# Preparing the second cross-attention's weights and first queries inside the latent stage of a decoder kernel

## Chip, cores and metric

The kernel runs on one core of one Trainium2 chip. The metric is the device time of one execution in microseconds, of which the median over the runs is taken.

## What is computed

Two decoder layers with a layer norm behind every sublayer, over 8 items of 112 tokens and 256 features, all in fp32. The stages in order: a state-space layer, a cross-attention of 16 heads, a mixture of experts, a latent attention, a wide cross-attention, and a last feed-forward with gated low-rank parts. The change touches the fourth and fifth:

```python
x = _layernorm(x + _L1_attn_ref(x, ...))      # latent attention, 16 heads of 16, causal
x = _layernorm(x + _L1_xattn_ref(x, ctx_768, Wq, Wk, Wv, Wo, bo))
x = _layernorm(x + _L1_ffn_ref(x, ...))

def _L1_xattn_ref(x, context, Wq, Wk, Wv, Wo, bo):   # context: 8 x 375 x 192
    q = (x @ Wq).reshape(B, Tq, 8, 128) * SCALE
    k = (context @ Wk).reshape(B, Tk, 8, 128) * SCALE
    v = (context @ Wv).reshape(B, Tk, 8, 128)
    attn = softmax(einsum('bqhc,bkhc->bhqk', q, k))
    return einsum('bqhk,bkhc->bqhc', attn, v).reshape(B, Tq, 1024) @ Wo + bo
```

## The kernel before, in words

Each stage is a function with one or two instruction blocks; at the end of a block all engines meet. Inside a block every engine has a program of its own and the engines wait for each other by counting semaphores. The order of work is written out by hand. The state lies in SBUF twice: `core.x` (tokens on partitions) and `core.xt` (features on partitions). There are eight PSUM banks of 512 fp32 columns.

**Latent attention** (`latent_attention`, L1881) has two blocks. The first (L1939 to L2015) makes latents, queries and keys with their rotations. SP sends queries and keys to DRAM and back into strips (`q_strips`, `k_strips`), one half of the items at a time (`rearrange`, L1905); GpSimd clears the strips first (L1942). The second block (L2040 to L2275) holds the attention in rounds: in round r TensorE makes the scores of item r+1 (banks 0 to 3, L2067 and L2073), turns the probabilities of item r (banks 5 and 6, L2086) and weighs its values (bank 7, L2095), and finishes item r−1: `turn_back` (L2102), `turn_output` (L2110), `out_projection` (L2115), all but the first in bank 4. `turn_state` (L2121) turns the normalized state of item r−2 back for `core.xt`. VectorE takes the maxima and subtracts them (`below_top`, L2161 and L2163), divides, adds the residual and normalizes (L2169 to L2190). ScalarE makes the exponentials (L2215), copies out of PSUM (L2220, L2225, L2230, L2241, L2247) and the deviation (L2235, L2236). Round −1 fills this pipeline, rounds 8 and 9 drain it. SP only sends the second half of the strips in this block, GpSimd sets the values' ones column and adds the output bias to the state (L2054).

**The wide cross-attention** (`wide_cross_attention`, L1057) multiplies no query or key projection per item. It folds the weights: per head, Wq times Wk turned into `w_a`, and Wv times Wo into `w_b`. For that the weights are turned first. TensorE prepares in two lists (L1073, L1074, run at L1313 and L1316):
- `first`: seven groups of turns (four of Wq, three of Wk), six groups of folds into `w_a` (L1192), and the six groups of the first queries (`w_a` times the state of items 0 and 1, L1222, by the helper at L86);
- then the first scores (`scores(0, 0)`, L1277 and L1280);
- `second`: three groups of turns of Wv (L1182), six groups of folds into `w_b` (L1201, L1205), and two groups of turns of the first context (L1225, L1228).

Each group fills one bank, alternately 0 and 7; ScalarE empties bank 0 (L1513, L1514) and VectorE bank 7 (L1375, L1376). A group is written only once the last one in its bank is copied. Then come 8 items of four units each (L1318). In a unit TensorE makes the scores of the following unit, turns probabilities (L1289) and does one or two small jobs in bank 0 (`jobs`, L1076): queries two items ahead, context turns, output projection (L1232), and the feed-forward's parts. VectorE makes the maxima (L1382) and normalizes; ScalarE makes the exponentials (L1521). GpSimd adds the output bias `bo` to the state at the stage's start (L1165), and VectorE waits for that (`bias_added`) before its first `normalize_heads`. SP loads two contexts, then the feed-forward's weights, then each further context two items ahead (L1151). The cross-attention weights themselves were loaded during the mixture stage (L1663).

The two-instruction count of fp32 matmuls in the rows (48 for 24 of them) is how the profile records them.

Of the kernel before, what the change touches and what calls it, by code (L numbers as in the profile page):

```python
# [7 lines left out]
F32 = mybir.dt.float32  # L8
# [8 lines left out]
N = B * T  # L17
# [13 lines left out]
INNER = 1024  # L31

# [97 lines left out]
class Core:  # L130
# [25 lines left out]
    def allocate_parts(self, ctx):  # L156
# [8 lines left out]
            {n: sbr(f"w{n}_{part}", [128, INNER]) for n in "kv"} for part in ("high", "low", "rest", "rest_low"))  # L165

# [890 lines left out]
def wide_cross_attention(core, d, output):  # L1057
# [44 lines left out]
    PRE = len(first) + len(second)  # L1102
    HALF = PRE // 2
    assert PRE % 2 == 0

    def pre_at(job_):
        return (first + second).index(job_)

    with ExitStack() as ctx:
        sb = lambda name, shape: ctx.enter_context(nc.sbuf_tensor(f"x{layer}_{name}", shape, F32))  # L1110
        pair = lambda name, shape: [sb(f"{name}{p}", shape) for p in range(2)]
        wq_t, wk_t, wv_t = sb("wq_t", [128, G, D]), sb("wk_t", [128, G, DC]), sb("wv_t", [128, G, DC])
        w_a, w_b = sb("w_a", [128, KD, M, 128]), sb("w_b", [128, M, D])
        ctx_t, cn = pair("ctx_t", [128, 2, SE]), pair("cn", [SP_, ST, DC])
        qt = pair("qt", [128, M, 2 * T])
# [7 lines left out]
        ctx_loaded = [sem("ctx_loaded0"), sem("ctx_loaded1")]  # L1123
        pre_ready, pre_used = [sem("pre_ready0"), sem("pre_ready1")], [sem("pre_used0"), sem("pre_used1")]
# [21 lines left out]
        PRE_BANK = [bank[0], bank[7]]  # L1146

        with nc.Block() as block:
            @block.sync
            def _(sp):  # L1150
                for i in range(B):  # L1151
                    if i == 2:
                        core.load_lora_weights(sp, d)
                    if i >= 2:
                        sp.wait_ge(s_ready, (i - 1) * J)
                    sp.dma_start(ctx_t[i % 2][:, :, :], d["ctx_t"][i].rearrange("(c p) n -> p c n", p=128)).then_inc(ctx_loaded[i % 2], 16)
# [12 lines left out]
            def _(pe):  # L1169
                ident = core.c(128, C_ID, 128)  # L1170

                def prepare(n, job_):

                    out, kind = PRE_BANK[n % 2], job_[0]
                    wait_past(pe, pre_used[n % 2], n // 2)
                    if kind == "turn":
                        _, name, c, g = job_
                        w = dict(q=core.wq, k=core.wk, v=core.wv)[name]
                        rows = 128 if name == "q" or c == 0 else CB
                        for k in range(512 // rows):  # L1180
                            h = 4 * g + k
                            last = pe.transpose(out[:, k * rows:(k + 1) * rows], w[0:rows, c, h * 128:(h + 1) * 128], ident[0:rows, 0:rows])  # L1182
                    elif kind == "fold_a":
                        _, c, g = job_
                        if c == 0 and g == 0:
                            for b in range(2):
                                pe.wait_ge(pre_used[b], (len(TURNS) + 1 - b) // 2)
                        cols = slice(0, 128) if g < 2 else slice(128, DC)
                        wide = cols.stop - cols.start
                        for k in range(512 // wide):  # L1190
# [3 lines left out]
                    elif kind == "fold_b":  # L1194
                        if job_[1] == 0:
                            for b in range(2):
                                pe.wait_ge(pre_used[b], (pre_at(job_) + 1 - b) // 2)
# [1154 lines left out]
```

## Time and profile before

| | |
|---|---|
| median of 3 runs | 1099.26 us (1098.34 to 1099.91) |
| profiled execution: its own time | 1098.13 us |
| its span in the profile | 1096.3 us |
| TensorE busy in the span | 998.7 us, 91% |
| VectorE, ScalarE, GpSimd busy | 586.3, 410.3, 150.6 us |
| mean granted clock of TensorE | 0.964 |

Times in the rows count from the span's start. In this execution the latent stage's first block begins near 671.1 us, its second near 694.4 us, and the wide cross-attention near 784.5 us. Busy time of TensorE is that of its matmuls, which overlap and whose ends are modelled; its granted clock is given as a share of 2.4 GHz, so 0.50 is 1.2 GHz. "Idle before" names what ended an engine's idle time.

### The profile page before, as it was taken

What the parts mean: (1) busy time and instruction counts of PE and PEld (TensorE: products, weight loads), DVE (VectorE), ACT (ScalarE), POOL (GpSimd) and SP (SyncE); (2) the same over time, 40 slices, a digit from 0 to 9 for tenths busy, and PEclk for the clock granted to TensorE, in tenths of its full rate; (3) what the DMA queues carried; (4) which work ended last, traced back from release to release, by engine and by line L of the source; (5) the groups of instructions that cost most, each with busy time, mean ns of one, the idle gap of its engine ahead of it and who ended that gap; (6) DMA issues with size and microseconds to landing.
All of it is one profiled execution on the core that took longest, in us unless ns stands there. A gap on an engine that the chain in (4) does not pass through costs nothing. (4 is left out here: it accounts for less than half of the span.)

```text
span 1096.3 us, 17961 instructions
## 1 busy us (share of the span) xinstructions
PE 998.7 (91%) x6656; PEld 773.7 (71%) x6656; DVE 586.3 (53%) x1319; ACT 410.3 (37%) x1065; POOL 150.6 (14%) x151
## 2 busy tenths in 40 slices
PE   6899699999999999869999996688789999999985
PEld 4578577777777777569999994355576776676563
DVE  2786545555555556656655554477325444544543
ACT  2556433333333334335444522366423222322221
POOL 0334311011011000014343422100100000000000
PEclk9999899999999999979999997899799999999997
DMA  4500000000000000074121000600100000001000
GB/s 146 186 2 1 29 15 1 16 15 1 14 0 0 0 0 0 1 242 117 46 70 38 0 1 1 135 1 2 46 1 15 15 15 15 14 2 27 4 6 13
DMA packets 24286, 34.34 MB, mean 31 GB/s; under 512 B 3168, under 2 KB 19888, under 8 KB 24224
## 3 DMA queue, kind: packets, MB, share of 16 engines
q1 hardware_dynamic: 24224, 33.51, 10.3%
q8 instruction: 39, 0.64, 0.2%
q14 instruction: 23, 0.19, 0.1%
HBM read 30.75 MB, written 2.75 MB: 31 GB/s over the span
## 5 line engine op out<-in xcount | busy, mean ns | idle before, releaser
L1028 ACT ACTIVATE x_prob<-bank,x_negmax 112x375 f32<-112x375 f32 x128 | 72.3, 570 | 153.2 <-DVE x_negmax L944 153.2
L1778 DVE TENSOR_TENSOR moe_h_low<-moe_sq,moe_h_high 128x448 fp32r<-128x448 f32 x64 | 54.8, 873 | 52.8 <-ACT moe_h_high L1843 39.6
L1819 POOL TENSOR_TENSOR moe_sq<-moe_r 128x448 f32<-128x448 f32 x64 | 64.2, 1005 | 122.3 <-ACT moe_r L1851 103.8
L86 PE MATMUL bank<-moe_w_low,moe_h_high 128*112 128x256 f32 x256 | 71.8, 281 | 0.0
L86 PE MATMUL bank<-moe_w_high,moe_h_high 128*112 128x256 f32 x256 | 71.7, 280 | 0.0
L86 PE MATMUL bank<-moe_w_high,moe_h_low 128*112 128x256 f32 x256 | 71.7, 280 | 0.0
L944 DVE TENSOR_REDUCE x_negmax<-bank 112x1 f32<-112x375 f32 x128 | 64.1, 543 | 7.7 <-PE bank L836 5.7
L1851 ACT ACTIVATE moe_r<-bank 128x448 f32<-128x448 f32 x64 | 35.0, 546 | 86.6 <-PE bank L86 84.9
L1521 ACT ACTIVATE x_prob<-bank,x_negmax 112x375 f32<-112x375 f32 x64 | 36.1, 569 | 76.4 <-DVE x_negmax L1382 76.4
L949 DVE COPY x_prob_t<-bank 125x336 f32<-125x336 f32 x128 | 59.0, 499 | 5.7 <-PE bank L845 3.8
L857 PEld LDWEIGHTS bank<-x_prob_t,x_v 125*64 125x64 f32 x768 | 37.2, 136 | 33.9 <-issue 29.9
L836 PE MATMUL bank<-x_kt,x_qt 64*112 64x375 f32 x256 | 56.8, 521 | 0.7 <-DVE x_kt L936 0.7
L845 PE MATMUL bank<-const,x_prob 112*125 112x112 f32 x384 | 53.7, 274 | 3.2 <-ACT x_prob L1028 3.0
L845 PEld LDWEIGHTS bank<-const,x_prob 112*125 112x125 f32 x384 | 50.3, 188 | 6.8 <-ACT x_prob L1028 5.4
L86 PE MATMUL bank<-moe_xt_high,moe_w_high 128*128 128x448 f32 x128 | 48.4, 378 | 4.2 <-DVE moe_w_low L1784 2.9
L86 PE MATMUL bank<-w_in,xt 128*112 128x512 f32 (+2 forms) x128 | 42.0, 467 | 11.1 <-DMA w_in<-in_L_attn_W_in 8.3
L857 PE MATMUL bank<-x_prob_t,x_v 125*64 125x112 f32 x768 | 50.8, 268 | 0.0
L810 POOL COPY x_inv<-x_inv_head 112x512 f32<-112x512 f32 x16 | 9.8, 615 | 281.5 <-DVE x_inv_head L955 281.5
L1277 PE MATMUL bank<-x_ctx_t,x_qt 128*112 128x375 f32 x128 | 46.7, 487 | 1.8 <-ACT x_prob L1521 1.0
L1382 DVE TENSOR_REDUCE x_negmax<-bank 112x1 f32<-112x375 f32 x64 | 32.1, 543 | 29.7 <-PE bank L1280 29.7
L86 PE MATMUL bank<-moe_xt_low,moe_w_high 128*128 128x448 f32 x128 | 47.4, 370 | 0.0
L86 PE MATMUL bank<-moe_xt_high,moe_w_low 128*128 128x448 f32 x128 | 47.3, 370 | 0.0
(360 smaller groups left out, 2281.0 us busy)
## 6 DMA issues: line engine op xcount, KB each, us to landing
moe_w<-in_L_ffn_W SPq DMA_DIRECT2D x16, 512.0 KB, 4.7
ctx_t<-in_ctx_t SPq DMA_DIRECT2D x8, 376.0 KB, 4.7
x_ctx_t<-in_ctx_t SPq DMA_DIRECT2D x8, 376.0 KB, 3.4
wk<-in_L_xattn_Wk SPq DMA_DIRECT2D x2, 1024.0 KB, 6.7
wv<-in_L_xattn_Wv SPq DMA_DIRECT2D x2, 1024.0 KB, 9.4
wq<-in_L_xattn_Wq SPq DMA_DIRECT2D x2, 1024.0 KB, 11.5
wo<-in_L_xattn_Wo SPq DMA_DIRECT2D x2, 1024.0 KB, 13.3
w_in<-in_L_attn_W_in SPq DMA_DIRECT2D x1, 1160.0 KB, 6.9
```

Source lines behind the costliest of these rows:

```text
L86: last = pe.matmul(out, lhs, rhs, start=(k == 0), stop=(k == len(pairs) - 1))
L836: last = pe.matmul(S_BANK(u, e)[0:T, 0:S], qt[p][rows, u, :], kt[p][rows, u, :], start=True, stop=True)
L845: last = pe.transpose(T_BANK(u, e)[0:SP_, k * T:(k + 1) * T], PROB(u, e)[:, k * SP_:(k + 1) * SP_], ident[0:T, 0:T])
L857: last = pe.matmul(bank[6 + u // HU][e * DH:(e + 1) * DH, at:at + T], v[p][:, k, g * DH:(g + 1) * DH], prob_t[u % 2][e][:, k, :], start=(k ...
L944: dve.tensor_reduce(negmax[:, g:g + 1], S_BANK(u, e)[0:T, 0:S], AX_X, ALU.max, negate=True).then_inc(max_ready, 1)
L949: dve.tensor_copy(prob_t[u % 2][e][:, :, :], T_BANK(u, e)[0:SP_, 0:ST * T] .rearrange("s (k t) -> s k t", k=ST)).then_inc(pt_copied, 1)
L1028: act.activation(PROB(u, e)[:, :], S_BANK(u, e)[0:T, 0:S], ACT.Exp, bias=negmax[:, g:g + 1], accum_out=total[:, g:g + 1]).then_inc(p_ready, 1)
L1277: pe.matmul(S_BANK[e][0:T, 0:S], q[:, 2 * j + e, query], c[:, 0, 0:S], start=True, stop=False)
L1521: act.activation(prob[w % 2][e][:, :], S_BANK[e][0:T, 0:S], ACT.Exp, bias=negmax[:, g:g + 1], accum_out=total[:, g:g + 1]).then_inc(e_read ...
L1778: dve.tensor_tensor(h_low[half][:, m, :], sq[m % 2][:, :], h_high[half][:, m, :].bitcast(F32), ALU.subtract).then_inc(low_done, 1)
L1819: pool.tensor_tensor(sq[m % 2][:, :], r[m % 2][:, :], r[m % 2][:, :], ALU.mult).then_inc(sq_done, 1)
L1851: act.activation(r[m % 2][:, :], bank[m][:, 0:HALF], ACT.Relu).then_inc(h_used, 1)
```

## The change

The turned and folded weights, both context tiles, the turned context and the first queries get a place that lasts over both stages (`allocate_folded`); the first queries lie in the memory of `q_strips`, which is dead behind the last latent scores. The two preparation lists and the two-bank scheme leave `wide_cross_attention`, which now starts with `scores(0, 0)`; its SP loads the feed-forward weights first and contexts from item 2 on. The latent stage gets 30 groups of extra work, numbered 0 to 29:
- 0 to 6, the turns of Wq and Wk: ahead of the second block's first scores, banks 5 and 6 in turn, copied by ScalarE (even numbers) and VectorE (odd);
- 7 to 12, the folds into `w_a`: in round 0, ahead of the scores of item 1, banks 5, 6 and 7 in turn, all copied by ScalarE, between its exponentials of item 0;
- 13 to 15, the turns of Wv: behind round 7's last weighing; 16 to 18 and 19 to 21, the folds into `w_b`: in round 8, before and behind `turn_output`; 22, 23 (first context) and 24, 25 (first queries) behind the last `out_projection`; 26 to 29, the other first queries, in round 9. All of these use banks 0 and 1, copied by ScalarE (even) and VectorE (odd).

The turn of the last item's state comes behind all of them. The two context loads are now the first thing that SP does in the latent stage's first block. The counts and shapes of the moved matmuls, turns and copies stay. The bodies of `prepare` and `empty_extra` are those of the removed functions and are left out where they say nothing of order.

```diff
+    def allocate_folded(self, ctx):
+
+        sb = lambda name, shape: ctx.enter_context(self.nc.sbuf_tensor("x1_" + name, shape, F32))
+        self.wq_t, self.wk_t, self.wv_t = sb("wq_t", [128, XG, D]), sb("wk_t", [128, XG, DC]), sb("wv_t", [128, XG, DC])
+        self.w_a, self.w_b = sb("w_a", [128, KD, XM, 128]), sb("w_b", [128, XM, D])
+        self.x1_ctx = [sb(f"ctx_t{p}", [128, 2, SE]) for p in range(2)]
+        self.x1_cn = [sb(f"cn{p}", [SP_, ST, DC]) for p in range(2)]
+        self.q_strips = ctx.enter_context(self.nc.sbuf_tensor("la_q_strips", [128, 4, N], F32))
+        self.first_queries = self.q_strips[:, :, :].rearrange("p g n -> p (g n)")[:, 0:XM * 2 * T].rearrange("p (m t) -> p m t", m=XM)
+        self.x1_ctx_loaded = [self.sem("x1_ctx_loaded0"), self.sem("x1_ctx_loaded1")]
...
-    TURNS = [("q", c, g) for c in range(KD) for g in range(2)] + [("k", 0, 0), ("k", 0, 1), ("k", 1, 0)]
-    FOLDS = [(c, g) for c in range(KD) for g in range(2)] + [(c, 2) for c in range(KD)]
-    first = [("turn", *t) for t in TURNS] + [("fold_a", *f) for f in FOLDS] + [(QUERY, 0, a) for a in range(6)]
-    second = [("turn", "v", 0, 0), ("turn", "v", 0, 1), ("turn", "v", 1, 0)] + [("fold_b", n) for n in range(6)] + [(CTX_MAIN, 0), (CTX_REST, 0)]
...
+        w_a, w_b, ctx_t, cn = core.w_a, core.w_b, core.x1_ctx, core.x1_cn
+        qt = [core.first_queries, sb("qt1", [128, M, 2 * T])]
...
-                for i in range(B):
-                    if i == 2:
-                        core.load_lora_weights(sp, d)
-                    if i >= 2:
-                        sp.wait_ge(s_ready, (i - 1) * J)
+                core.load_lora_weights(sp, d)
+                for i in range(2, B):
+                    sp.wait_ge(s_ready, (i - 1) * J)
...
-                    if number[job_] == 0:
-                        pe.wait_ge(pre_used[0], HALF)
-                    else:
-                        pe.wait_ge(job_used, number[job_])
+                    wait_past(pe, job_used, number[job_])
...
-                pe.wait_ge(core.xw_loaded, 80 * (layer + 1))
-                for n, job_ in enumerate(first):
-                    prepare(n, job_)
                 scores(0, 0)
-                for n, job_ in enumerate(second):
-                    prepare(len(first) + n, job_)
                 for i in range(B + 2):
                     for u in range(J):
...
-                def prepared(n, job_):
-                    if n % 2 == 1:
-                        dve.wait_ge(pre_ready[1], n // 2 + 1)
-                        empty(job_, PRE_BANK[1], copy).then_inc(pre_used[1], 1)
-
-                for n, job_ in enumerate(first):
-                    prepared(n, job_)
                 row_max(0, 0)
                 dve.wait_ge(bias_added, 1)
-                for n, job_ in enumerate(second):
-                    prepared(len(first) + n, job_)
                 normalize_heads(0, 0)
                 for i in range(B + 1):
                     for u in range(J):
...
                     act.wait_ge(end_log_ready, i + 1)
                     act.activation(end_rstd[:, i, :], end_rstd[:, i, :], ACT.Exp, scale=-0.5).then_inc(end_rstd_ready, 1)
...
                 act.preload_act_table_set(EXP_LN)
-                for n, job_ in enumerate(first):
-                    prepared(n, job_)
                 exps(0, 0)
-                for n, job_ in enumerate(second):
-                    prepared(len(first) + n, job_)
...
+                    for i in range(2):
+                        sp.dma_start(core.x1_ctx[i][:, :, :], d["ctx_t"][i].rearrange("(c p) n -> p c n", p=128)).then_inc(core.x1_ctx_loaded[i], 16)
                     sp.wait_ge(strips_cleared, 1)
...
+            turns = [("turn", "q", c, g) for c in range(KD) for g in range(2)] + [
+                ("turn", "k", 0, 0), ("turn", "k", 0, 1), ("turn", "k", 1, 0)]
+            folds = [("fold_a", c, g) for c in range(KD) for g in range(2)] + [("fold_a", c, 2) for c in range(KD)]
+            value_turns = [("turn", "v", 0, 0), ("turn", "v", 0, 1), ("turn", "v", 1, 0)]
+            value_folds = [("fold_b", n) for n in range(6)]
+            first = [("context", 0), ("context", 1)] + [("query", a) for a in range(6)]
+            extra = turns + folds + value_turns + value_folds + first
+            AHEAD, FILL = len(turns), len(turns) + len(folds)
+            TAIL_V, TAIL_F = FILL + len(value_turns), FILL + len(value_turns) + len(value_folds)
+
+            def place(n):
+
+                if n < AHEAD:
+                    return 5 + n % 2, ("act", "dve")[n % 2]
+                if n < FILL:
+                    return 5 + n % 3, "act"
+                return n % 2, ("act", "dve")[n % 2]
+
+            def evicted(engine, n):
+
+                return sum(1 for k in range(n) if place(k)[1] == engine)
...
+                    def wait_evicted(n):
+
+                        for engine in ("act", "dve"):
+                            wait_past(pe, pre_used[engine], evicted(engine, n))
+
+                    def prepare(n):
+
+                        job, (b, _) = extra[n], place(n)
+                        out = bank[b]
+                        if n == FILL:
+                            pe.wait_ge(m_ready, NG * B)
+                        before = [k for k in range(n) if place(k)[0] == b]
+                        if before:
+                            engine = place(before[-1])[1]
+                            pe.wait_ge(pre_used[engine], evicted(engine, before[-1] + 1))
+                        if n in (AHEAD, TAIL_V, TAIL_F):
+                            wait_evicted(n)
...
+                        elif job[0] == "query":
+                            if job[1] == 0:
+                                pe.wait_ge(nt_copied, 2)
...
+                        last.then_inc(pre_ready, 1)
+
+                    def prepare_all(a, b):
+                        for n in range(a, b):
+                            prepare(n)
+
+                    pe.wait_ge(core.xw_loaded, 160)
+                    prepare_all(0, AHEAD)
                     pe.wait_ge(wo_loaded, 48)
                     for r in range(-1, B + 2):
+                        if r == 0:
+                            prepare_all(AHEAD, FILL)
                         if there(r + 1):
                             scores(r + 1)
                         if there(r - 1):
                             turn_back(r - 1)
-                        if there(r - 2):
+                        if there(r - 2) and r <= B:
                             turn_state(r - 2)
+                        if r == B:
+                            prepare_all(TAIL_V, TAIL_V + 3)
+                        if r == 0:
+                            wait_evicted(FILL)
                         if there(r):
                             turn(r, 0)
                             turn(r, 1)
...
                             turn(r, 2)
                             weigh(r, 1)
                         if there(r - 1):
+                            if r == B:
+                                prepare_all(TAIL_V + 3, TAIL_F)
                             out_projection(r - 1)
+                            if r == B:
+                                prepare_all(TAIL_F, TAIL_F + 4)
                         if there(r):
                             turn(r, 3)
                             weigh(r, 2)
...
                             values(r + 1)
                         if there(r):
                             weigh(r, 3)
+                        if r == B - 1:
+                            prepare_all(FILL, TAIL_V)
+                        if r == B + 1:
+                            prepare_all(TAIL_F + 4, len(extra))
+                            turn_state(B - 1)
 
...
+                    empty_extras(0, AHEAD)
                     for r in range(-1, B + 1):
                         if there(r + 1):
                             below_top(r + 1, 0)
+                        if r == B:
+                            empty_extras(FILL, TAIL_V)
                         if there(r - 1):
                             divide(r - 1)
                         if there(r + 1):
                             below_top(r + 1, 1)
                             below_top(r + 1, 2)
                             below_top(r + 1, 3)
+                        if r == B:
+                            empty_extras(TAIL_V, TAIL_F)
                         if there(r - 1):
                             residual(r - 1)
                             normalize(r - 1)
+                    empty_extras(TAIL_F, len(extra))
...
+                    def empty_extras(a, b):
+                        for n in range(a, b):
+                            if place(n)[1] == "act":
+                                act.wait_ge(pre_ready, n + 1)
+                                empty_extra(n, copy).then_inc(pre_used["act"], 1)
+
+                    empty_extras(0, AHEAD)
                     for r in range(-1, B + 2):
                         if there(r - 1):
                             copy_weighed(r - 1)
-                        if there(r - 2):
+                        if r == B:
+                            empty_extras(FILL, TAIL_V)
+                        if there(r - 2) and r <= B:
                             copy_state(r - 2)
                         if there(r):
                             copy_turned(r, 0)
                         if there(r + 1):
                             exps(r + 1, 0)
+                        if r < 0:
+                            empty_extras(AHEAD, AHEAD + 1)
                         if there(r):
                             copy_turned(r, 1)
+                        if r == B:
+                            empty_extras(TAIL_V, TAIL_V + 3)
                         if there(r - 1):
                             copy_output(r - 1)
                         if there(r + 1):
                             exps(r + 1, 1)
+                        if r < 0:
+                            empty_extras(AHEAD + 1, AHEAD + 3)
                         if there(r):
                             copy_turned(r, 2)
                         if there(r + 1):
                             exps(r + 1, 2)
+                        if r < 0:
+                            empty_extras(AHEAD + 3, AHEAD + 4)
                         if there(r):
                             copy_turned(r, 3)
                         if there(r + 1):
                             exps(r + 1, 3)
+                        if r < 0:
+                            empty_extras(AHEAD + 4, FILL)
+                        if r == B:
+                            empty_extras(TAIL_V + 3, TAIL_F)
                         if there(r - 1):
                             deviation(r - 1)
                         if there(r + 1):
                             copy_values(r + 1)
+                        if r == B:
+                            empty_extras(TAIL_F, len(extra))
+                            copy_state(B - 1)
...
-        latent_attention(core, d)
-        wide_cross_attention(core, d, out)
+        with ExitStack() as second:
+            core.allocate_folded(second)
+            latent_attention(core, d)
+            wide_cross_attention(core, d, out)
```

## Rows read from the trace of the kernel before

**Rows 1.** The page, part 1: busy time, share of the span, instructions.

```profile
PE 998.7 (91%) x6656; PEld 773.7 (71%) x6656; DVE 586.3 (53%) x1319; ACT 410.3 (37%) x1065; POOL 150.6 (14%) x151
```

**Rows 2.** Windows by stage: length, busy us per engine, TensorE clock, DMA share, GB/s.

```profile
694.45:713.76 19.31, 12.34 (x125) 7.87 (x125) 9.44 (x16) 7.46 (x14) 5.18 (x5) 0.73 0.51 97
713.76:775.44 61.68, 53.09 (x650) 36.49 (x646) 42.67 (x103) 40.01 (x98) 0.00 (x0) 0.97 0.01 2
775.44:784.55 9.11, 3.94 (x14) 2.19 (x14) 2.74 (x10) 3.08 (x10) 0.00 (x0) 0.67 0.00 1
...
811.85:823.72 11.87, 10.04 (x56) 7.35 (x54) 4.37 (x7) 3.93 (x9) 0.00 (x0) 0.86 0.00 1
823.72:1096.30 272.58, 249.94 (x1275) 174.48 (x1274) 129.35 (x399) 72.84 (x252) 0.00 (x0) 0.97 0.05 13
```

**Rows 3.** Timeline of the wide stage's start: start, length, engine, line, operation.

```profile
784.58 4.52 POOL L1165 TENSOR_TENSOR x<-x,bo 112x2048 f32<-112x2048 f32 x1 [84.89 <-POOLq L2040]
784.59 3.87 PE L1182 MATMUL bank<-const,wq 128*128 128x128 f32 x16 [0.69 <-PEq L2040]
...
791.26 7.64 PE L1192 MATMUL bank<-x_wk_t,x_wq_t 128*128 128x128 f32 x64 [0.72 <-ACT x_wk_t L1513]
...
809.62 1.48 PE L1277 MATMUL bank<-x_ctx_t,x_qt 128*112 128x375 f32 x4 [0.67 <-issue]
...
811.97 1.00 DVE L1382 TENSOR_REDUCE x_negmax<-bank 112x1 f32<-112x375 f32 x2 [3.87 <-PE bank L1280]
...
813.11 0.57 ACT L1521 ACTIVATE x_prob<-bank,x_negmax 112x375 f32<-112x375 f32 x1
...
823.72 1.51 PE L1277 MATMUL bank<-x_ctx_t,x_qt 128*112 128x375 f32 x4
```

**Rows 4.** Timeline of the start of the latent rounds.

```profile
694.45 1.28 ACT L2209 ACT_TABLE_LOAD   x1 [0.27 <-PEq L1939]
...
696.62 1.71 PE L2067 MATMUL bank<-la_hide,la_ident 112*112 112x448 bf16 x4 [4.57 <-DMA la_k_strips<-la_keys]
...
700.18 0.62 DVE L2161 TENSOR_REDUCE la_top<-bank 112x4 f32<-112x448 f32 x1 [6.66 <-PE bank L2073]
...
705.09 1.74 PE L2067 MATMUL bank<-la_hide,la_ident 112*112 112x448 bf16 x4 [4.38 <-DVE la_masked L2163]
...
713.76 0.96 PE L2067 MATMUL bank<-la_hide,la_ident 112*112 112x448 bf16 x4
...
715.77 0.63 DVE L2161 TENSOR_REDUCE la_top<-bank 112x4 f32<-112x448 f32 x1 [2.24 <-PE bank L2073]
```

**Rows 5.** Timeline of the last weighing and the drain behind it.

```profile
775.04 0.40 PE L2095 MATMUL bank<-la_prob_t,la_v 112*32 112x112 f32 x8 [0.29 <-ACT la_prob_t L2220]
...
775.99 0.41 DVE L2190 TENSOR_SCALAR la_normed<-la_res,la_mv,la_rstd 112x256 f32<-112x256 f32 x1 [0.51 <-ACT la_rstd L2236]
...
776.43 0.65 PE L2102 MATMUL bank<-const,la_weighed 128*112 128x128 f32 x4 [0.99 <-ACT la_weighed L2225]
...
778.73 2.05 PE L86 MATMUL bank<-la_wo,la_ot 128*112 128x256 f32 x4 [0.43 <-ACT la_ot L2230]
...
782.50 0.20 ACT L2236 ACTIVATE la_rstd<-la_rstd 112x1 f32<-112x1 f32 x1
...
783.94 0.35 ACT L2247 COPY xt<-bank 128x224 f32<-128x224 f32 x1 [0.29 <-PE bank L2121]
```

**Rows 6.** Groups by form on TensorE, 784 to 824 us.

```profile
L86 PE MATMUL bank<-xt,x_w_a 128*128 128x224 f32 x48 | 9.3, 354 | 0.7 <-issue 0.7
...
L1192 PE MATMUL bank<-x_wk_t,x_wq_t 128*128 128x128 f32 x32 | 4.0, 280 | 0.7 <-ACT x_wk_t L1513 0.7
...
L1192 PE MATMUL bank<-x_wk_t,x_wq_t 128*128 128x64 f32 x32 | 3.8, 276 | 0.0
```

**Rows 7.** Windows of TensorE alone: length, busy us, clock, DMA share, GB/s.

```profile
812.00:816.00 4.00, 2.44 (x20) 1.00 0.00 0
816.00:819.00 3.00, 3.00 (x9) 0.50 0.02 5
```

More of the change, by code:

```diff
@@ L31 @@
 INNER = 1024
+XG = 8
+XM = XG + XG // 2
 E0, F0, FM = 8, 512, 4
@@ L1101, in wide_cross_attention @@
         number[job_] = len(number)
[L1102 to L1107, printed above, removed]
     with ExitStack() as ctx:
@@ L1145, in wide_cross_attention @@
         JOB, S_BANK, T_BANK, U_BANK = bank[0], bank[1:3], bank[3:5], bank[5:8]
-        PRE_BANK = [bank[0], bank[7]]
         with nc.Block() as block:
@@ L1170, in _ @@
                 ident = core.c(128, C_ID, 128)
[L1172 to L1190, printed above, removed]
-                            h = (4 * g + k) % G
-                            last = pe.matmul(out[:, k * wide:(k + 1) * wide], wq_t[:, h, c * 128:(c + 1) * 128], wk_t[:, h, cols],
-                                             start=True, stop=True)
[L1194 to L1197, printed above, removed]
-                        for k in range(2):
-                            at = 2 * job_[1] + k
-                            if at < G:
-                                last = pe.matmul(out[:, k * D:(k + 1) * D], wv_t[:, at, 0:128], core.wo[:, at, :], start=True, stop=True)
-                            else:
-                                for e in range(2):
-                                    h = 2 * (at - G) + e
-                                    last = pe.matmul(out[e * CB:(e + 1) * CB, k * D:(k + 1) * D], wv_t[:, h, 128:DC], core.wo[:, h, :],
-                                                     start=True, stop=True)
-                    else:
-                        if kind == QUERY and job_[2] == 0:
-                            for b in range(2):
-                                pe.wait_ge(pre_used[b], (n + 1 - b) // 2)
-                        if kind == CTX_MAIN:
-                            pe.wait_ge(ctx_loaded[0], 16)
-                        last = work(out, job_)
-                    last.then_inc(pre_ready[n % 2], 1)
@@ L1268, in scores @@
                         pe.wait_ge(ctx_loaded[i % 2], 16 * (i // 2 + 1))
-                        if i == 0:
-                            for b in range(2):
-                                pe.wait_ge(pre_used[b], (len(first) + 1 - b) // 2)
-                        elif i % 2 == 0:
+                        if i > 0 and i % 2 == 0:
                             pe.wait_ge(job_used, number[(QUERY, i // 2, 4)] + 1)
@@ L1296, in weigh @@
                     wait_past(pe, ot_dve, 2 * i + half)
-                    if i == 0:
-                        for b in range(2):
-                            pe.wait_ge(pre_used[b], HALF)
-                    elif half == 0:
+                    if i > 0 and half == 0:
                         pe.wait_ge(job_used, number[(CTX_MAIN, i)] + 1)
```

96 lines of the change are left out of this document (71 added, 25 removed).

## The prediction

> **What bounds the kernel now.** I read the page first: TensorE is busy 91% of the span [rows 1], so a gain can only come from its idle time or from time at its lower clock. The windows by stage say where that is [rows 2]. Behind 823.72 us the second cross-attention keeps TensorE busy 249.94 of 272.58 us, and nothing there is touched. In the latent stage's repeating rounds (713.76 to 775.44 us) it is busy 53.09 of 61.68 us. Ahead of the rounds it is busy only 12.34 of 19.31 us at a mean clock of 0.73, and in the drain behind the last round 3.94 of 9.11 us at 0.67. Then come 39.17 us (784.55 to 823.72 us) of preparation in the next stage, ahead of its first round. The reader is to see two holes beside a block of work that needs TensorE and depends on little.
>
> The timeline of that block [rows 3]: seven groups of turns until 790.54 us, six folds of the query weights (7.64 us), six first queries, the first scores at 809.62 us, then the value turns, value folds and context turns until the second scores at 823.72 us. The first softmax (maxima from 811.97 us, exponentials until 813.68 us) lies under the value turns. I take the second scores as the anchor: from there the code of the stage is the same in both kernels.
>
> **What goes.** Between the last weighing of the latent stage (it ends at 775.44 us [rows 5]) and the anchor lie 48.28 us. The sum compares this distance with the new one and charges the delay ahead of the rounds apart.
>
> **Ahead of the rounds: seven turns.** The set-up before the latent rounds ends as the one at 784.5 us does, with a ScalarE table load at 694.45 us [rows 4]; the turns follow at once, with the same two banks and the same pair of copying engines. I price them as they ran: from 784.59 to 790.54 us, 5.95 us [rows 3]. So the first scores leave at about 700.5 us instead of 696.62 us, where they had waited 4.57 us for the key strips [rows 4]: +3.85 us. The two context loads go ahead of everything on SP's queue, at the stage's very start, where SP would only wait for the strips to be cleared and then for the projections; nothing is late behind them, so I take 0.
>
> These first scores ran at the low clock, since TensorE had idled before them: 3.56 us from their start to VectorE's first reduction, against 2.01 us for the same work from 713.76 to 715.77 us at full clock [rows 4]. Six microseconds of turns stand before them now; in the old place such turns were enough, for the folds right behind them ran at their best pace from the first to the last [rows 3, 6]. I take the high clock, −1.55 us, and keep 0 as the other end.
>
> **Ahead of the second scores: six folds.** They take 7.64 us at full clock [rows 3, 6]. VectorE meanwhile works through the first item; in the old kernel TensorE waited 4.38 us for it [rows 4]. New order: scores until 702.6, values until 703.3, folds until 710.9 us, second scores straight behind, 2.0 us at full clock, first reduction at 712.9 us. VectorE's four steps and then the third scores follow as before: the old second scores left at 705.09 us and, slow too, gave the reduction its start 3.56 us later; from there to the third scores at 713.76 us it is 5.1 us. So the third scores leave at 718.0 us. **The front costs 4.2 us**; 5.8 us if the first scores stay slow. Bounds: 1 us if turns and folds hide better, 14 us if folds and both scores run at the low clock (7.6 and 3.1 us more). I take 4.2, since the row nearest in kind, the folds behind their own turns, was at the high clock. ScalarE alone empties these banks now, three of them in turn. In the old block two banks and two engines let the folds run without a break, so one engine with three banks should keep up; its exponentials slip by one copy, which nobody waits for, as the next item's maxima come only after 712 us.
>
> A rule is weighed here. The rows show 16 folds of 128 columns in 4.0 us and 16 of 64 columns in 3.8 us (each two instructions [rows 6]): half the columns bought almost nothing. The Trainium skill (TensorE: Matmul & The Clock Gate, section Back-to-back issue gap) gives a gap that falls with the columns; by it the narrow folds would cost half, and the front some 1.9 us less. The rows decide.
>
> **Rounds.** Nothing is added in rounds 0 to 6; I take 0. The old rounds had TensorE waiting for VectorE and ScalarE in short pieces, and these stay.
>
> **Behind the rounds.** Everything counts from T, the end of the last weighing. Work now in the drain:
> - value turns, value folds and context turns: as between the first and second scores, 10.04 us busy out of 11.87 us [rows 2]. This contains a fall of the clock to 0.50 from 816 to 819 us at least [rows 7]: the 3 us of work done in it would have taken 1.5 us at full clock, so it cost 1.5 us, which I leave in as the price of one such fall.
> - six first queries: 9.32 us [rows 6].
> - the drain's own steps at full clock: 0.65 us for turning the weighed values back (four transposes [rows 5]), estimated from it 0.4 us each for the two-transpose steps (state, output, last state), 1.0 for the output projection (2.05 us at the low clock): 2.9 us.
> - waits that this order makes. The third value turn waits for VectorE, which first normalizes item 6 (until T+0.96) and then copies: 0.6 us. The first query needs the bank that holds the context turns, whose copy ScalarE makes only behind the last deviation. That comes 1.92 us after the projection's end (780.78 to 782.70 us [rows 5]) and the copy 0.5 us more; 1.1 us of context turns cover part: 1.4 us idle.
> - last copy 0.35 and the stage's boundary 0.30 us (783.94 to 784.59 us [rows 3, 5]): 0.7 us with the semaphore.
> Sum: 10.04 + 9.32 + 2.9 + 2.0 + 0.7 = 25.0 us, so the second cross-attention starts at T+25.0 instead of T+9.1.
> Then its first scores (809.62 to 811.91 us, 2.29 us), and now bare the first softmax (to 813.68 us, 1.77 us behind the scores' end, and a semaphore), since nothing lies beside it: 4.1 us. Anchor at **T+29.1, against T+48.28: 19.2 us gained**. Bounds: 14 us with two more falls of the clock and slow queries at the start, 22 us with none. GpSimd's bias addition (4.52 us [rows 3]) was under 39 us of preparation; it ends 0.5 us behind the exponentials now, and VectorE's first normalization waits for it behind its queue; the turn that needs it comes 3.9 us after the anchor, so 0, and at most 0.5.
>
> **Sum.** −19.2 + 4.2 = −15.0 us. The profiled execution took 1098.13 us (span 1096.3), so 1083.1 us; the median of the runs is 1.13 us above it, which gives 1084.3 us.
>
> **Rivals.**
> 1. *The front runs at the low clock.* TensorE's turns there stop for copies, and the first two stand about 1 us until the table load is over. For it: the clock fell behind the value turns, in which TensorE had kept stopping for copies (busy 2.44 of the 4 us before the fall [rows 7]); against it: in the old block it rose behind the same turns. Price: folds +7.6, two scores +3.1: 1095 us. Beside it: the Trainium skill (same page, section A second HAM failure mode: psum-queue depth-cycling) says that pauses between groups that cycle through PSUM banks make the clock swing; the fall at 816 us agrees, and by this rule the time would lie between 1084 and 1095 us. Chance 0.12.
> 2. *The holes hide more.* The drain runs without a fall of the clock and the value turns fit round their copies (−3), and the folds start early (−1.5): 1080 us or a little less. For it: the fall at 816 us followed stalls for copies that the fuller order of the drain may cover. Chance 0.10.
> 3. *Slower.* The low clock holds through all the moved work, front and drain. The work is the same wherever it stands, so each microsecond of it that is run at 1.2 instead of 2.4 GHz takes one more; it decides from 15 us of such work. All of it (folds 7.6, scores 3.1, drain about 22) gives 1084 + 33 = 1117 us. Against it: the value work, stalls and all, had a mean clock of 0.86 in the old place [rows 2]. Chance 0.03.
> 4. *No change.* The rounds take the gain back, because ScalarE's late copies shift every exponential, 1.9 us in each of eight rounds. Against it: only round 0 holds added copies, and the later rounds' order is untouched. 1099 us, chance 0.02.
>
> **Numbers.** My case, a gain between 9 and 19 us, has 0.73. The range takes the price bounds of front and drain together, 1080 to 1090 us: it leaves out most of rivals 1, 3 and 4, some of rival 2. Against about 0.2% that a measurement of this kernel can tell, faster 0.95, same 0.02, slower 0.03.
>
> **What would show it.** The latent stage's first scores near 700.5 us and its third near 718; rounds of unchanged pace; from the last weighing 25 us to the next stage's table load; there the first scores at once, then 1.8 us idle on TensorE, and nothing changed behind the anchor. A mean clock under 0.9 from 702 to 713 us would be rival 1. Wrong altogether would be rounds that lengthen, or a gap on TensorE of over 2 us in the drain.

## The result and the profile after

The changed kernel takes 1088.70 us in the median of four runs (1081.28 to 1089.54), the kernel before 1099.41 us beside it: ratio 0.988, 95% interval 0.984 to 0.992. The forecast was 1084.3 us (1080 to 1090). The profiled execution of the changed kernel took 1089.54 us, with a span of 1087.7 us: 8.6 us less span than before, where 15.0 us was forecast.

The page, part 1, of the changed kernel, beside [rows 1]:

```profile
PE 1000.9 (92%) x6656; PEld 775.4 (71%) x6656; DVE 584.4 (54%) x1316; ACT 411.1 (38%) x1068; POOL 150.5 (14%) x151
```

The same number of TensorE instructions, 2 us more busy time in a shorter span: no work went away, and some of it ran slower. The windows by stage say where (columns as in [rows 2]):

```profile
0.00:673.05 673.05, 626.99 (x4338) 516.12 (x4338) 383.84 (x763) 268.84 (x660) 133.95 (x141) 0.97 0.12 38
673.05:696.45 23.40, 20.81 (x54) 9.99 (x54) 7.94 (x13) 7.08 (x12) 6.89 (x4) 0.89 0.52 112
696.45:719.55 23.10, 21.19 (x220) 16.73 (x220) 11.51 (x19) 13.01 (x24) 5.20 (x5) 0.92 0.42 81
719.55:781.23 61.68, 53.07 (x651) 36.02 (x648) 42.67 (x103) 39.66 (x98) 0.00 (x0) 0.98 0.01 2
781.23:805.90 24.67, 21.61 (x116) 18.02 (x116) 8.33 (x19) 7.09 (x18) 0.00 (x0) 0.93 0.00 1
805.90:810.15 4.25, 2.31 (x9) 0.90 (x9) 1.00 (x2) 2.50 (x5) 4.22 (x1) 1.00 0.44 111
810.15:1087.70 277.55, 254.89 (x1274) 177.59 (x1274) 129.10 (x398) 72.93 (x252) 0.28 (x1) 0.96 0.04 12
```

Read against [rows 2], line by line. The start of the latent rounds took 23.10 us instead of 19.31: +3.8. The rounds took 61.68 us in both. From the last weighing to the second scores it was 24.67 + 4.25 = 28.92 us instead of 48.28: −19.4. That is −15.6 us, and what was moved did what it should. Two stretches that the change does not touch took the rest back: +2.0 us ahead of the latent rounds (696.45 against 694.45 us), and +5.0 us behind the second scores (277.55 against 272.58 us), where TensorE was busy 5.0 us longer with one instruction fewer in the record. The same instructions at a lower clock is what that looks like. Windows of TensorE alone in that stretch (columns as in [rows 7]):

```profile
810.00:812.00 2.00, 1.85 (x6) 0.82 0.01 3
812.00:814.00 2.00, 2.00 (x6) 0.50 0.00 0
814.00:816.00 2.00, 2.00 (x12) 0.83 0.00 0
912.00:914.00 2.00, 1.08 (x4) 0.92 0.56 178
914.00:916.00 2.00, 2.00 (x7) 0.50 0.00 0
1062.00:1064.00 2.00, 1.20 (x4) 0.97 0.00 0
1064.00:1066.00 2.00, 2.00 (x6) 0.50 0.00 0
```

Three falls to 1.2 GHz. Matmuls take up to twice as long in them (1.74 instead of 0.96 us for the same four in the rows further down), so each costs up to 1.7 us, and together they account for the 5.0 us. The kernel before had none there: its clock was 1.00 from 823.72 to 1082 us. The second fall stands behind a pause that the kernel before has too, of the same length (first line before, second after), with no fall behind it; so it is with the pauses of 1.14 and 1.18 us ahead of the third:

```profile
924.90 0.68 PE L1238 MATMUL bank<-lora_b,x_gm_t 64*112 64x256 f32 x2 [1.14 <-ACT xt L1513]
```

```profile
912.92 0.68 PE L1189 MATMUL bank<-lora_b,x_gm_t 64*112 64x256 f32 x2 [1.14 <-ACT xt L1428]
```

The first fall stands right behind the second scores, behind the softmax that the change laid bare:

```profile
805.90 1.28 ACT L1468 ACT_TABLE_LOAD   x1 [0.37 <-PEq L1993]
805.93 4.50 POOL L1160 TENSOR_TENSOR x<-x,bo 112x2048 f32<-112x2048 f32 x1 [104.22 <-POOLq L1993]
805.94 1.49 PE L1222 MATMUL bank<-x_ctx_t,la_q_strips 128*112 128x375 f32 x4 [0.79 <-PEq L1993]
...
808.29 1.00 DVE L1306 TENSOR_REDUCE x_negmax<-bank 112x1 f32<-112x375 f32 x2 [2.67 <-PE bank L1225]
...
810.15 1.77 PE L1222 MATMUL bank<-x_ctx_t,la_q_strips 128*112 128x375 f32 x4 [1.90 <-ACT x_prob L1436]
```

These answer to [rows 3]. TensorE stands 1.90 us for the exponentials ("1.90 <-ACT x_prob"), then its four score matmuls take 1.77 us instead of 1.51. Start and drain, the rows that answer to [rows 4] and [rows 5]:

```profile
702.64 0.96 PE L2020 MATMUL bank<-la_hide,la_ident 112*112 112x448 bf16 x4
...
705.13 7.36 PE L2107 MATMUL bank<-x_wk_t,x_wq_t 128*128 128x128 f32 x64
...
712.32 0.92 PE L2020 MATMUL bank<-la_hide,la_ident 112*112 112x448 bf16 x4
...
719.55 1.74 PE L2020 MATMUL bank<-la_hide,la_ident 112*112 112x448 bf16 x4
...
793.41 0.46 ACT L2299 COPY x_cn<-bank 125x384 f32<-125x384 f32 x1
...
793.93 11.03 PE L88 MATMUL bank<-xt,x_w_a 128*128 128x224 f32 x48 [1.37 <-ACT x_cn L2299]
```

The reader is to see first scores and folds at full clock, folds without a break, and the wait ahead of the queries, 1.37 us for one copy that ScalarE made behind the last deviation. The queries then took 11.03 us instead of 9.32, since the clock fell near their start (0.55 from 794 to 796 us). Two more falls are in these rows. The turns in the front ran in part at the low clock, as most of them had in the old place (0.50 from 784.55 to 788.70 us); the clock was back 0.6 us before the first scores. And the third scores, the first work of the rounds, took 1.74 us instead of the 0.96 of [rows 4]. The turns as a whole, TensorE alone:

```profile
696.45:702.64 6.19, 5.32 (x33) 0.72 0.76 211
```

Two theories for the 7 us went into the experiments. **A:** the rises and falls of the clock keep a time of their own, each run meets them at other points of the program, and a gap on TensorE costs its length plus, often, a fall behind it. **B:** either a fixed consequence of the change, or chance that no order of the work can influence.

### The profile page after: what moved, and what is told of

Read it like the earlier page. It is cut to its first block and busy times, and to the rows that moved or that the text cites. A ratio compares the mean times of both kernels' runs of the same rounds, so it can differ in the third digit from the quotient of the medians.

```text
span 1087.7 us, 17961 instructions
## 1 busy us (share of the span) xinstructions
PE 1000.9 (92%) x6656; PEld 775.4 (71%) x6656; DVE 584.4 (54%) x1316; ACT 411.1 (38%) x1068; POOL 150.5 (14%) x151
## 5 line engine op out<-in xcount | busy, mean ns | idle before, releaser
L88 PE MATMUL bank<-x_w_b,x_ot 128*112 128x256 f32 x192 | 45.2, 393 | 0.5 <-DVE x L1372 0.5
```

What stands on the lines that cost most here:

```text
L88: last = pe.matmul(out, lhs, rhs, start=(k == 0), stop=(k == len(pairs) - 1))
```

## Experiments

The kernels ran in sets, each set beside the kernel before on one chip. Means are over all runs of a kernel; single runs of one kernel spread by 4 to 15 us, so the means and intervals carry the comparisons.

**The changed kernel again.** No edit.

> The changed kernel once more, to see how its runs spread: three of its first four runs took 1088.3 to 1089.5 us and one 1081.3. Theory A (where TensorE's clock falls differs from run to run, since its rises and falls keep a time of their own that each run meets at another point): runs anywhere between 1080 and 1090 us, the profile with falls at other places than 805.2, 916 and 1063 us counted from the span's start, and a span shorter or longer by the work that the falls slow. Theory B (the change itself makes the falls behind it): all runs within 1 us of 1089 and the falls at the same places.

Seven runs: 1082.27 to 1090.72 us, median 1088.52, ratio 0.990 (0.987 to 0.993). Beside them the kernel before took 1095.22 to 1105.08 us over 21 runs. The first three runs of the kernel before, within 1.6 us of each other, had hidden a spread of 10 us. Both kernels spread, so B's "all within 1 us" falls. (The expectation's 805.2 us is no fall of the first trace; from the drain on they begin at 794.2, 811.3, 913.7 and 1063.9 us.) The profile (span 1080.5 us) has a front of 22.87 us and 27.23 us from the last weighing to the second scores: no fall in the queries this time. It has none in the rounds either, and they took 60.26 us instead of 61.68:

```profile
718.79:779.05 60.26, 51.70 (x651) 35.18 (x648) 42.64 (x103) 39.77 (x98) 0.00 (x0) 1.00 0.01 2
```

So the equal 61.68 us before and after hold one fall each, near 768 us before and near 719 us after. The falls near 914 and 1063 us are gone here. But right behind the start of the second scores (806.28 us) the clock fell again, and that one fall accounts for the stretch behind (274.2 against 272.6 us):

```profile
802.08:806.28 4.20, 2.30 (x8) 1.00 0.49 111
806.28:811.00 4.72, 4.72 (x13) 0.64 0.01 2
811.00:1060.00 249.00, 236.35 (x1233) 1.00 0.04 12
```

**Only the front, only the drain.**

```diff
 front_only: the latent stage's list of groups
-            value_turns = [("turn", "v", 0, 0), ("turn", "v", 0, 1), ("turn", "v", 1, 0)]
-            value_folds = [("fold_b", n) for n in range(6)]
-            first = [("context", 0), ("context", 1)] + [("query", a) for a in range(6)]
+            value_turns, value_folds, first = [], [], []
             extra = turns + folds + value_turns + value_folds + first
 tail_only: these three lines stay, and behind them
+            turns, folds, first = [], [], [("context", 0), ("context", 1)]
```

The groups that are not in the list are made in the wide stage, in banks 0 and 7, at their old places.

> Only the seven turns and six folds move into the latent stage; first queries, value turns, value folds and the first context stay in the wide stage. Their 15.0 us (784.59 to 799.63 us in the old trace) go, the rounds start 3.8 us later as in the changed kernel: 11.2 us faster than before, 1088 us, if the two ends add up. If the drain's part carried the gain instead: 1094 us or more. The clock may add or take 1.7 us per fall.

> Only the value turns, value folds and the first context move, into the drain; turns, folds and first queries stay in the wide stage ahead of its first scores. 11.9 us go, the bare softmax comes back with 1.9 us, and the drain grows by some 5 us, since its own waits hide a good part of the work: 5 us faster than before, 1094 us. If the drain hid nothing: no gain at all, 1099 to 1101 us.

Front only: mean 1091.0 us of eight runs, ratio 0.992 (0.989 to 0.995), by its intervals the larger part of the gain. In its trace the start of the rounds took 22.93 us (+3.6) and the way to the second scores 33.05 us (−15.2): 11.6 us gained on the path, as expected (11.2); the whole time gained 9.6 us in the mean, so the 1088 us forecast was missed by 3. Drain only: mean 1098.0 us of ten runs, ratio 0.998 (0.996 to 1.000), which the runs can't tell from no change; on the path 42.62 instead of 48.28 us, −5.7, as expected (5), but the whole time gained only 2.6 us in the mean: 1094 us was expected, and where the rest went the runs do not show. The two parts add up to −17.3 us on the path, against −15.6 in the first trace of the whole change and −17.5 in the trace just above, which has no fall in the queries.

**The copy ahead of the deviation.**

```diff
 ScalarE, round 8:
-                            empty_extras(TAIL_V + 3, TAIL_F)
+                            empty_extras(TAIL_V + 3, TAIL_F + 1)
                         if there(r - 1):
                             deviation(r - 1)
...
-                            empty_extras(TAIL_F, len(extra))
+                            empty_extras(TAIL_F + 1, len(extra))
```

> The changed kernel, but ScalarE copies the first context group ahead of the last deviation instead of behind it. In the changed kernel's trace TensorE stood 1.37 us for that copy, and its clock then fell from 794.9 to 798.3 us in the midst of the queries (worth 1.7 us). If the stall is all there is: 1.3 us faster than the changed kernel. If the stall is what makes the clock fall: 3 us faster. If the drain is bound elsewhere (the last state's chain): no change.

Mean 1085.7 us of six runs, ratio 0.986 (0.983 to 0.989), 2.3 us below the changed kernel on the same chip, which the spread of both leaves open (about ±2.8 us). The copy now runs under VectorE's steps behind the residual, and the queries start without the wait; a shorter one comes in among them, 0.43 us of the weight load for VectorE's copy of the second context group, which the third line shows:

```profile
795.55 0.48 ACT L2299 COPY x_cn<-bank 125x384 f32<-125x384 f32 x1 [1.83 <-PE bank L2130]
...
796.08 1.21 PE L88 MATMUL bank<-xt,x_w_a 128*128 128x224 f32 x5
...
797.94 7.49 PEld L88 LDWEIGHTS bank<-xt,x_w_a 128*128 128x128 f32 x40 [0.43 <-DVE x_cn L2226]
```

From the last weighing to the second scores it is 26.32 us: 0.9 us less than in the one trace of the changed kernel without a fall in the queries (27.23), 2.6 less than in the three with one (28.92 each). So the stall cost 0.9 us instead of the 1.3 expected, for that shorter wait, and 1.7 us more where the clock had fallen. The wait of 1.37 us was followed by a fall in the queries in four of the five traces that have it (the changed kernel's, and `filler` below), and none of the three without it (this one, `cover` twice) has a fall there: likely its doing, not proven by so few.

**Work, or something in its place, under the first softmax.** `cover` is the kernel above with two groups of value folds moved behind the wide stage's first scores. `filler` is the changed kernel with useless work there:

```diff
 filler, wide stage, TensorE:
                 scores(0, 0)
+                for n in range(12):
+                    pe.transpose(bank[7][:, n % 4 * 128:(n % 4 + 1) * 128], ident, ident)
```

> The order of order_fix, and the last two groups of value folds (1.95 us of matmuls) stand behind the wide stage's first scores instead of in the drain. Theory A (a gap on TensorE costs its length and, through the clock behind it, up to 1.7 us more): the softmax of 1.9 us is covered again, the fall of the clock that stood right behind it in three of three traces of the new arrangement (811.6, 806.9 and 811.3 us) is gone, 3 to 3.5 us faster than order_fix, mean near 1083 us. Theory B (only the gap's length counts, the falls are chance): 1.9 us faster than order_fix.

> The changed kernel with twelve transposes of the identity into a bank that nobody reads, right behind the wide stage's first scores; they do nothing but keep TensorE busy for some 1.6 us of the 1.9 us in which it stands for the first softmax. Theory A: no fall of the clock at that place, 1.7 us faster than the changed kernel although more work is done. Theory B (the falls come whatever TensorE does): the same time as the changed kernel, or slower by a few tenths.

`cover`: mean 1081.0 us of five runs, ratio 0.981 (0.979 to 0.984), 4.7 us below the kernel above (measured in another set of runs, about ±2.5 us), more than the 1.9 us of theory B, and above the 3 to 3.5 of A, which lies within the spread. On the path it gained 1.95 us (24.37 instead of 26.32), just the work that left the drain. `filler`: mean 1086.8 us of five runs, 0.986 (0.984 to 0.989); 1.2 us below the changed kernel's overall mean of 1088.0, with overlapping runs, so its time alone would settle nothing. Its trace does. TensorE's windows over the first softmax and behind the second scores, of `filler`, and then the same of the first trace of the changed kernel:

```profile
806.63:810.84 4.21, 3.77 (x21) 1.00 0.51 107
810.84:815.78 4.94, 4.94 (x25) 1.00 0.01 5
```

```profile
805.94:810.15 4.21, 2.31 (x9) 1.00 0.44 112
810.15:815.10 4.95, 4.95 (x14) 0.66 0.00 0
```

In the same 4.9 us behind the second scores TensorE got through 25 instructions instead of 14. The programs differ in the twelve transposes alone, with which TensorE was busy 3.77 instead of 2.31 us in the 4.21 us before. This is one trace of `filler` against four of the changed kernel.

**The kernel before and the changed kernel once more, for their traces.**

> The kernel before once more, for a second profile of it: its time of 1095 to 1105 us over 21 runs should show in the unchanged stages. Theory A: the stages ahead of the latent rounds (694.45 us in the first trace) and behind the second scores (272.58 us) both differ by 0 to 5 us, in steps that go with falls of the clock; the preparation in between stays 48.3 us within 2 us. Theory B: all stretches as in the first trace.

> The changed kernel a third time, for its profile: from its last weighing to the second scores 27.2 to 29 us, its front 22.9 to 23.1 us, whatever its whole time; a fall of the clock within 2 us of the second scores, if the bare softmax is what makes it. If the falls there are chance, none now.

The kernel before: 671.36 us to the latent stage (671.14 in the first trace), 48.28 us from the last weighing to the second scores, 272.60 us behind them. All stretches as in the first trace, so this trace speaks for B. The changed kernel: 1095.94 us, the slowest of its 18 runs. Its front took 22.88 us and its way to the second scores 28.92 us; but the part up to the latent stage, the same code in both kernels, took 679.24 us:

```profile
0.00:679.24 679.24, 632.31 (x4338) 519.51 (x4338) 382.86 (x763) 268.39 (x661) 133.66 (x142) 0.96 0.12 38
```

The same 4338 TensorE instructions as in the first trace after (673.05 us), busy 5.3 us longer: most of the 6.2 us is the clock's. And behind the second scores it fell again (0.66 over 4.95 us).

**The best version beside the changed kernel.**

> The version with the first softmax covered and the copy ahead of the deviation, a second time, beside the changed kernel on the same chip. Theory A: 7 us faster than the changed kernel in the mean (drain and first softmax 4.5 us, the rest falls of the clock), no fall within 5 us behind the second scores in its profile. Theory B: 3.2 us faster (1.3 and 1.9 us), and a fall there as often as in the changed kernel.

> The changed kernel a fourth time, as the partner of cover2. Mean near 1088 us, single runs from 1081 to 1096 us; in its profile a fall of the clock right behind the second scores (theory A), or none (theory B).

On one chip: `cover` 1080.4 us in the mean of five runs (1078.95 to 1082.29), ratio to before 0.983 (0.981 to 0.984); the changed kernel 1087.5 us of six (1081.37 to 1090.54), ratio 0.988 (0.985 to 0.991). The difference is 7.0 us, as A had it; with so few runs it is known to about 4 us, which does not quite exclude B's 3.2. Over all their runs it is 1088.0 us (18) against 1080.7 (10), 7.3 us with some ±2.1, and that does. Windows of `cover`, the drain and all behind the second scores:

```profile
780.18:800.30 20.12, 18.29 (x100) 15.65 (x100) 7.64 (x18) 6.61 (x17) 0.00 (x0) 1.00 0.00 1
804.54:1077.20 272.66, 249.93 (x1274) 174.47 (x1274) 129.59 (x399) 73.26 (x253) 0.30 (x1) 0.97 0.04 13
```

The drain is at full clock, and the stretch behind takes 272.66 us as in the kernel before. The changed kernel's trace from the same chip has 28.92 us to the second scores and 277.51 us behind them, as in its first.

The fall right behind the second scores, over all traces: in all five with a bare softmax in the full arrangement (the changed kernel four times, and the one with the copy moved), in none of the three with something under it (`filler`, `cover` twice). In the drain-only kernel the softmax is bare too, and there it did not come, though TensorE's work before it was the same (busy 2.33 of 4.24 us). Nor did it come in the three traces in which the value work covers the softmax (the kernel before twice, and the front-only kernel). That is five of six with the softmax bare and none of six with it covered: a gap makes a fall likely there, not certain. Of theory A that part stands. That the clock keeps a time of its own fits the places that change from run to run, but no run tells it from B's chance.

## Why the prediction was right or wrong

**Ahead of the rounds: right.** 4.2 us was forecast, 3.8 measured (3.6 to 3.8 in all traces of kernels that have it). The turns ended where the sum put them, the first scores and folds ran at full clock, the folds (7.36 us) without a break with ScalarE alone copying. Rival 1, folds and scores at the low clock, did not come. The folds took 7.36 us against 7.64 in the old place: no 1.9 us went with the narrower half. The Trainium skill (TensorE: Matmul & The Clock Gate, section Back-to-back issue gap) gives the gap that falls with the columns for one matmul by itself, and says that it comes out too small for few columns in a stream of weight loads and matmuls. This case's trace agrees with that: 32 instructions of 128 columns took 3.8 us and 32 of 64 columns 3.7 us, so it was the prediction's reading of the section that was too simple.

**The drain: right in sum.** T+25.0 us was forecast for the next stage's start and T+29.1 for the second scores; it was T+24.7 and T+28.9 in three of four traces. In the fourth, without a fall, the stage started at T+23.0, where the sum less its 1.5 us for a fall gives 23.5. The wait ahead of the queries was forecast at 1.4 us and was 1.37, the wait of the third value turn at 0.6 and was 0.85. The one fall of the clock that the sum took along from the value folds came in the queries instead, behind that wait.

**Rounds and GpSimd's addition: right.** 61.68 us before and after, each with one fall of the clock; 60.26 us without one. The addition ended at 810.43 us, 0.28 us behind the start of the second scores, and delayed nothing on TensorE.

**Behind the anchor: the step that failed.** "From there the code of the stage is the same in both kernels", and so its time was taken as the same. It took 277.5 us in three of four traces and 274.2 in one, instead of 272.6. Up to 1.7 us of that is the fall behind the bare softmax, which I had priced at the 1.77 us of the gap alone. The sum had put one fall of the clock into the drain and none behind it. The other two falls there (near 914 and 1063 us) and the 2.0 us ahead of the latent stage have no place in the sum. Together the stretches outside its terms took 7.0 us in the first trace. The range had 5.7 us of room on that side, put there for front and drain; that the median lies within it is therefore in part luck. The two late falls came in three of four traces of the changed kernel and at other places in the kernel with the copy moved and in one of the two of `cover`, and `filler` and the two partial kernels had one late fall each; whether the change makes them likelier than they were is not settled, with two traces of the kernel before, both without them. No experiment was aimed at them, nor at the 2.0 us: the part up to the latent stage took 671.1 to 671.5 us in the three traces without the front's part of the change (the kernel before twice, drain only) and 672.0 to 679.2 us in the nine with it. Why is open.

**The reference point.** The sum was made against one execution and moved by 1.13 us to a median of three runs within 1.6 us. Over 45 runs the kernel before takes 1100.6 us in the mean (1095.2 to 1105.1), the changed kernel 1088.0 us over 18 (1081.3 to 1095.9): 12.5 us, between the forecast 15.0 and the 10.7 of the first medians. "About 0.2%" as the bound of what can be told from no change was too narrow for a few runs of this kernel, which spread by 0.9%.

**Bounds.** The front's upper bound was put at 14 us, where its own terms give 4.2 + 7.6 + 3.1 = 14.9. And 1080 to 1090 us is not what the bounds of front and drain give together: −22 + 1 and −14 + 14 us would be about 1078 to 1099 us.

The rule named beside rival 1 (the Trainium skill, TensorE: Matmul & The Clock Gate, section A second HAM failure mode: psum-queue depth-cycling: short pauses between groups that cycle through banks make the clock swing) was a right worry, mostly at another place. Behind the first pauses of the front's turns the clock did fall (0.50 from 698.65 to 702.05 us), as it had fallen near there in the old kernel, where TensorE stood idle; but it was back before the scores and the folds. The falls in the drain and at the next stage's start followed single gaps of 1.37 us and 1.90 us.

## What to carry to other kernels

Where work moves out of a preparation into idle time, look at what it covered in its old place: here one softmax came out bare, for 1.9 us, and the fall of the clock that followed it in most traces took up to 1.7 us more. Two small groups left behind to cover it, and one copy put ahead of a wait on the same engine, gave 7 us more, over half as much again as the change itself. Compare such versions by the same stretch of their traces (from one event to another) before comparing their times, when the rest of the kernel spreads by more than what is looked for.

## What was not expected of the hardware

Runs of one kernel differed by 10 us (before, 45 runs) and 15 us (changed, 18 runs). The part up to the latent stage, identical in all kernels, took between 671.1 and 679.2 us in the traces, with 4338 TensorE instructions each time. Their busy time was 623.66 us in the shortest and 632.31 us in the longest, but it does not always go along: 624.80 and 624.88 us stand beside 671.36 and 672.95 us, and the remaining 1.6 us have no cause here. The falls of the granted clock stand at different points of the program from run to run, and where fewer of them meet TensorE's work a run is faster, by up to 1.7 us for each. Outside the two gaps studied above, whether a given pause is followed by a fall looks like chance in these traces: the same pause of 1.14 us was followed by one in three traces of the changed kernel, and not in the fourth.
